# A two-layer graph kernel: layer 1's self connection four pairs later, and eight groups' bases that stay in SBUF

## What is computed

```python
x = layernorm(x + L0_gnn(x, a, src, dst, edge_attr_4, edge_attr_64, ...))
x = layernorm(x + L1_gnn(x, a, edge_attr_16, edge_attr_4, src, dst, ...))

# inside L1_gnn
sc = concat([x0 @ Wsc0 * a * inv8, einsum(x1, Wsc1) * a * inv32])  # self connection, every node
e0, e1 = f0[edge_src], f1[edge_src]                                # gather per edge
...                                                                # messages from edge weights
n = segment_sum(message, edge_dst) / cnt                           # scatter to nodes
return sc + alpha * conv                                           # conv, alpha from n
```

## Time and profile before

| | us |
|---|---|
| median of 3 runs | 2022.29 |
| the runs | 2023.46, 2022.29, 2012.63 |
| profiled execution, its time | 2024.94 |
| profiled execution, its span | 2023.2 |
| stage 1, about | 0 to 722 |
| stage 2, about | 722 to 1048 |
| stage 3, about | 1048 to 1760 |
| stage 4, about | 1760 to 2023 |

### The profile page before, as it was taken

How to read it: one execution, slowest core, us unless ns; L and a number is a source line. 1 busy time by engine, 2 the same in 40 slices (tenths; PEclk the granted TensorE clock), 3 DMA queues, 4 the chain that set the end, 5 groups by cost and what they waited for, 6 DMA issues and landing times.

```text
span 2023.2 us, 47391 instructions
## 1 busy us (share of the span) xinstructions
PE 1423.3 (70%) x10327; PEld 1269.9 (63%) x10327; DVE 1445.6 (71%) x5762; ACT 1059.0 (52%) x3502; POOL 1473.4 (73%) x1925
## 2 busy tenths in 40 slices
PE   5888778887878668888868998898988888100000
PEld 4777677776767557667637888888888888100000
DVE  6767667776766459999955666666666666099998
ACT  3434434444433239999954554554454544056666
POOL 3777777777777548888864677777777777478886
PEclk9989988899988889999978999999999999555555
DMA  9877787777774379999944777777777776499997
GB/s 354 233 190 194 189 192 178 184 177 187 176 177 86 38 233 344 337 339 338 340 154 126 174 172 162 173 163 166 169 167 168 168 167 144 92 362 401 403 395 290
DMA packets 257604, 440.09 MB, mean 218 GB/s; under 512 B 33838, under 2 KB 131792, under 8 KB 257360
## 3 DMA queue, kind: packets, MB, share of 16 engines
q1 hardware_dynamic: 143920, 303.31, 44.1%
q0 software_dynamic: 75264, 67.79, 24.4%
q10 hardware_dynamic: 38304, 67.91, 9.1%
HBM read 235.60 MB, written 203.27 MB: 217 GB/s over the span
## 4 chain that ended last, share of the span: by engine, by line
POOL 28%; issue 20%; DVE 12%; PE 10%; DMA 7%; ACT 6%; ACTq 1%; DVEq 1%; another core or an unknown queue 1%; POOLq 0%; SPq 0%
POOL table L563 14%; POOL xg L538 8%; DVE stats L1186 4%; DVE res L1147 3%; DMA table<-sums,row_all 3%; ACT y L938 3%; POOL half_rstd L602 3%; DMA xg<-x_rows,src_all 2%; DVE res L1136 1%; DMA xg<-in_x_rows,src_all 1%; PE ps L711 1%; PE ps L731 1%; PE ps L697 1%; PE ps L713 1%
## 5 line engine op out<-in xcount | busy, mean ns | idle before, releaser
L563 POOL DMA_INDIRECT table<-sums,row_all x392 | 631.8, 1612 | 254.7 <-issue 143.2
L938 ACT ACTIVATE y<-res,norm 128x160 f32<-128x160 f32 x756 | 330.3, 507 | 129.6 <-POOL norm L604 72.8
L873 ACT COPY msg<-ps 128x192 f32<-128x192 f32 (+1 forms) x196 | 57.6, 294 | 576.4 <-PE ps L731 348.5
L538 POOL DMA_INDIRECT xg<-in_x_rows,src_all x196 | 200.2, 1022 | 86.3 <-issue 55.4
L1096 DVE SCALAR_TENSOR_TENSOR x1g<-ps,a_all,x1g 128x160 f32<-128x160 f32 x392 | 132.4, 379 | 163.0 <-PE ps L752 133.2
L538 POOL DMA_INDIRECT xg<-x_rows,src_all x196 | 195.3, 996 | 64.2 <-issue 59.4
L1186 DVE BATCH_NORM_STATS2 stats<-res 128x6 f32<-128x160 f32 x784 | 196.0, 312 | 3.8 <-issue 0.3
L1052 DVE TENSOR_TENSOR pe<-ps,ea_all 128x192 f32<-128x192 f32 x196 | 70.1, 357 | 173.2 <-ACT msg L873 98.4
L661 PE MATMUL ps<-ident,xg 128*128 128x128 f32 x392 | 87.3, 306 | 147.2 <-ACT xz L860 108.8
L711 PE MATMUL ps<-weights,midT 128*128 128x128 f32 (+1 forms) x784 | 164.3, 293 | 35.0 <-DVE msg L1057 23.3
L602 POOL TENSOR_TENSOR half_rstd<-var,minus_half 128x8 f32<-128x8 f32 x98 | 164.7, 1680 | 14.2
(11 more groups left out here) (127 smaller groups left out, 4462.6 us busy)
## 6 DMA issues: line engine op xcount, KB each, us to landing
table<-zeros SPq DMA_DIRECT2D x98, 384.0 KB
tab<-table SPq DMA_DIRECT2D x98, 384.0 KB, 5.2
table<-zeros SPq DMA_DIRECT2D x49, 648.0 KB
tab<-table SPq DMA_DIRECT2D x98, 324.0 KB, 5.4
xzT<-in_xzT SPq DMA_DIRECT2D x98, 320.0 KB, 5.0
x1g<-x_rows SPq DMA_DIRECT2D x98, 320.0 KB
base_rows<-x1g SPq DMA_DIRECT2D x98, 320.0 KB
x1g<-base_rows SPq DMA_DIRECT2D x98, 320.0 KB, 5.0
```

What stands on the lines that cost most here:

```text
L538: pool.indirect_dma_start(out=xg[j % RING][:, t, 0:width], out_offset=None, in_=rows, in_offset=bass.IndirectOffsetOnAxis(ap=src_all[:, at ...
L563: pool.indirect_dma_start(out=table[l], out_offset=bass.IndirectOffsetOnAxis(ap=row_all[:, at:at + 1], axis=0), in_=sums[j % 4][:, t, 0:W] ...
L938: last = nc.scalar.activation(y[u][:, t, :], res[u][:, t, :], ACT.Identity, scale=rstd[u][:, t:t + 1], bias=shift[u][:, t:t + 1])
```

## The change

In stage 3 the self connection's parts get a lag four steps greater on every engine: on PE `nodes1a` and `nodes1b` 6 for 2 and `turn1a` and `turn1b` 5 for 1, on ACT `copy_z1` 4 for 0 and `copy_nTa`, `copy_nTb` 5 for 1, on DVE `add_self_a`, `add_self_b` 6 for 2, on SP `load_x1` 4 for 0 and `store_base` 8 for 4. `store_base` leaves out groups 90 to 97: their bases are left in the eight `x1g` buffers. The last stage takes the groups in the order 96, 97, 90 to 95, then 0 to 89 (`at_last`), so that item m uses the buffer its group already lies in; `load_base` leaves out the first eight items, and `table_row1` waits for these on the self connection's last count in place of a load. ACT's list of the last stage is written out for 18 steps at each end, for 10 before.

```diff
+def at_last(m):
+    if isinstance(m, int) and m < RING:
+        return NG - 2 + m if m < 2 else NG - RING + m - 2
+    return m - RING
...
                 def store_base(g, m, u):
+                    if isinstance(m, int) and m >= NG - RING:
+                        return
...
-                    run_stages(sp, base, NP, 10, [(10, pair_landed), (4, store_base), (0, load_x1),
+                    run_stages(sp, base, NP, 10, [(10, pair_landed), (8, store_base), (4, load_x1),
                                                   (0, load_attr), (0, load_dst_row)], RING)
...
                 def load_base(g, m, u):
+                    if isinstance(m, int) and m < RING:
+                        return
...
-                                 base_rows[bass.ds(m * GROUP, GROUP), :]...
+                                 base_rows[bass.ds(at_last(m) * GROUP, GROUP), :]...
...
                     for u in range(RING):
-                        sp.wait_ge(s_bstore[u], landed(2 * NG - RING + (u - 2 * NG) % RING, first_of(u, RING), RING))
+                        sp.wait_ge(s_bstore[u], 16 * len(range(first_of(u, RING), 2 * NG - RING, RING)))
                     run_stages(sp, NG, NG, 10, [(0, load_base), (2, load_table)], RING)
...
-                    run_stages(pe, NP, NP, 10, [(1, first_map), (0, hidden), (1, edge_weights), (2, nodes1a), (0, turn_x),
-                                                (1, turn1a), (3, second_map), (2, turn_mid), (1, turn1b),
-                                                (2, nodes1b), (5, sum_pair)], RING)
+                    run_stages(pe, NP, NP, 10, [(1, first_map), (0, hidden), (1, edge_weights), (6, nodes1a), (0, turn_x),
+                                                (5, turn1a), (3, second_map), (2, turn_mid), (5, turn1b),
+                                                (6, nodes1b), (5, sum_pair)], RING)
...
                     run_stages(act, NP, NP, 10, [(0, copy_z), (1, copy_h), (0, hidden_act), (0, copy_xT),
-                                                 (1, copy_nTa), (3, copy_message), (2, copy_midT), (0, copy_z1),
-                                                 (1, copy_nTb), (5, copy_sums)], RING)
+                                                 (5, copy_nTa), (3, copy_message), (2, copy_midT), (4, copy_z1),
+                                                 (5, copy_nTb), (5, copy_sums)], RING)
...
-                run_stages(act, l * NG, NG, 10 if l else 18, ([(8, normalise), (9, store), (0, gates)] if l == 0 else [(9, store), (8, normalise)]), RING)
+                run_stages(act, l * NG, NG, 18, ([(8, normalise), (9, store), (0, gates)] if l == 0 else [(9, store), (8, normalise)]), RING)
...
-                        (4, message_vectors), (2, compare), (4, message_sum), (2, add_self_a), (1, products), (2, add_self_b)], RING)
+                        (4, message_vectors), (2, compare), (4, message_sum), (6, add_self_a), (1, products), (6, add_self_b)], RING)
...
                 def table_row1(g, m, u):
-                    dve.wait_ge(s_base[u], landed(g, first_of(u, RING), RING))
+                    if isinstance(m, int) and m < RING:
+                        dve.wait_ge(s_z1, 2 * NG)
+                    else:
+                        dve.wait_ge(s_base[u], landed(g - RING, first_of(u, RING), RING))
```

More of the change, by code:

```diff
@@ L472, in load_base @@
                     sp.dma_start(x1g[u][:, :, :].rearrange("p t c -> p (t c)"),
-                                 base_rows[bass.ds(m * GROUP, GROUP), :].rearrange("(p t) c -> p (t c)", t=T)).then_inc(s_base[u], 16)
+                                 base_rows[bass.ds(at_last(m) * GROUP, GROUP), :].rearrange("(p t) c -> p (t c)", t=T)).then_inc(s_base[u], 16)
                 def load_table(g, m, u):
@@ L486, in load_table @@
                     sp.dma_start(tab2[u // 2][:, u % 2, 0:T * W],
-                                 table[l][bass.ds(m * GROUP, GROUP), :].rearrange("(p t) c -> p (t c)", t=T)).then_inc(s_nx[u], 16)
+                                 table[l][bass.ds((at_last(m) if l else m) * GROUP, GROUP), :].rearrange("(p t) c -> p (t c)", t=T)).then_inc(s_nx[u], 16)
                 def store_last():
@@ L494, in store_last @@
                         sp.wait_ge(s_yrest, SHARED * l + m - (NG - SHARED) + 1)
-                        sp.dma_start(to[m * GROUP:(m + 1) * GROUP, :].rearrange("(p t) c -> p (t c)", t=T),
+                        n = at_last(m) if l else m
+                        sp.dma_start(to[n * GROUP:(n + 1) * GROUP, :].rearrange("(p t) c -> p (t c)", t=T),
                                      y[u][:, :, :].rearrange("p t c -> p (t c)")).then_inc(s_store[u], 16)
@@ L613, in factor @@
                     pool.wait_ge(s_q2, g + 1 - NG)
-                    tt(q[:, 1, :, :], a_all[:, bass.ds(m - 1, 2), :], q[:, 1, :, :], ALU.mult).then_inc(s_q3, 2)
+                    tt(q[:, 1, :, :], a_all[:, bass.ds(at_last(m) - 1, 2), :], q[:, 1, :, :], ALU.mult).then_inc(s_q3, 2)
                     pool.wait_ge(s_q3, g + 1 - NG)
@@ L949, in store @@
                     to = x1_rows if l == 0 else out
-                    act.dma_start(to[bass.ds(m * GROUP, GROUP), :].rearrange("(p t) c -> p (t c)", t=T),
+                    act.dma_start(to[bass.ds((at_last(m) if l else m) * GROUP, GROUP), :].rearrange("(p t) c -> p (t c)", t=T),
                                   y[u][:, :, :].rearrange("p t c -> p (t c)")).then_inc(s_store[u], 16)
-                run_stages(act, l * NG, NG, 10 if l else 18, ([(8, normalise), (9, store), (0, gates)] if l == 0 else [(9, store), (8, normalise)]), RING)
+                run_stages(act, l * NG, NG, 18, ([(8, normalise), (9, store), (0, gates)] if l == 0 else [(9, store), (8, normalise)]), RING)
         @block.vector
```

## The result

| | before | after |
|---|---|---|
| median, us (12 runs each) | 2016.86 | 2006.06 |
| runs, us | 2006.83 to 2028.18 | 1996.94 to 2011.11 |
| profiled execution, its time | 2024.94 | 2009.39 |
| its span | 2023.2 | 2007.6 |

A forecast was written before the change was run, and what follows sets the result against it. It took POOL's scatters to pace stage 3 and ACT the last stage; 7.5 + 3.8 + 0.2 = 11.5 us off 2024.94 gave 2013.4, less 2.65 for the runs' median 2010.8, said as 2011, range 2000 to 2021.

The forecast's parts named there:

- Start of the last stage: Border of stages 3 and 4: two tables load first instead of after four bases, DVE starts 3.8 us earlier.
- Start of stage 3: Ahead of POOL's first scatter: less self connection work lets it start 7.5 us earlier, bounds 2.7 to 19.3.
- the 6.5 us: PE's self connection work taken out of the steps of pairs 2 to 5 ahead of the first sum, counted in full.
- unnamed waits: ACT's waits at stage 3's start with no cause in the profile, 10.8 us in sum; expected to stay, over by 1074.
- the unknown part: Stage 3's start, ahead of PE's steps: x1 loads moved behind and ACT's waits; 0 to 12.8 us, taken as 1.0.
- First to last scatter: Stage 3 from POOL's first scatter to its last: 660.7 us should stand, within 5.
- Last stage: ACT bounds it at 2.53 us a group; eight base loads fewer give nothing, more written-out groups 0.2 us.
- The unnamed waits going with the copies: Rival, stage 3's start: ACT's waits vanish with the moved copies, 17 to 19 us there, 2000 us in all; chance 0.12.
- The DMA engines as the bound: Rival, last stage: DMA engines set the pace, so fewer base loads give 6.5 us more, 2004.5; chance 0.06.
- More collisions: Rival, stage 3: among the first ten pairs five more scatters wait 1.7 us, 8.5 us back, 2019; chance 0.08.
- a slow jump of ACT's loop: Rival, last stage: ACT's loop waits at its jump back in each of ten rounds, 34 us, 2045; chance 0.06.
- The small gain at stage 3's start: Rival: PE's half clock and the gather burst eat all but 0 to 3 us there, 2017 in all; chance 0.18.

The follow-up runs named there:

- bases_only: Changed kernel with the self connection's lags set back, the last stage still taking eight groups' bases from SBUF; ratio to the kernel before 0.999.
- before_again: Kernel before plus one line: POOL waits for ACT's copy of pair j-2 at gathers 3 to 7 of stage 3; ratio to the kernel before 0.995.
- short_burst: Changed kernel with POOL waiting for PE at five pairs' gathers of stage 3, so 8 instead of 18 leave together; ratio to the kernel before 0.9886.
- the repeat: Changed kernel run once more as it is; ratio to the kernel before 0.9947, first to last scatter 639.3 us.
- no_base_loads: Changed kernel without any load of a base in the last stage; ratio to the kernel before 0.9929, last stage 240.2 us.
- late_store: Changed kernel with ACT issuing each store of the last stage one group later; ratio to the kernel before 0.9918.

## Why the prediction was right, and where it was off

**The size.** 11.5 us foreseen, 11.5 measured by the ratio (7.7 to 15.3). That is 0.57%, little above the 0.5% that was to count as faster, and the interval (0.38 to 0.76%) holds that limit. But the terms that the experiments bear out come to 4.5 + 4.3 = 8.8 us: the agreement to a tenth is luck, that it lies in the interval is not. The time itself, 2006.06, lies 5 us under the 2011 foreseen and just inside the forecast's own range, since the kernel before has 2016.86 as its median over 12 runs where the prediction started from 2022.29 over 3.

**Start of the last stage**, 3.8 us with bounds 3.4 to 4.6: 3.95 in the two profiles, 4.3 between the kernel before and bases_only. The working holds: two tables in front instead of four bases, DVE 4.75 us after the landing (4.9 foreseen). The prediction weighed a fixed 2.0 us plus the bytes at 436 GB/s (the Trainium skill, DMA: Bandwidth & Descriptors, Anatomy of one DMA; the section gives this fit for transfers that GpSimd issues, and these are SyncE's), an estimate of 3.5 us for two tables. By the same fit one table, 0.33 MB, is an estimate of 2.8 us, and the first landed 2.73 us after its issue (1748.38 to 1751.11). The second table landed 4.1 us after the first was issued (1748.38 to 1752.48), but with six table loads issued in 2.70 us, not two, so it does not separate the two estimates.

**Start of stage 3**, 7.5 us with bounds 2.7 to 19.3: 4.3. This is the term that was mis-sized. The step that failed is "PE runs without a gap through nearly all of these steps, so I count them in full", together with PE's lower clock, which the prediction named as a cost of up to 3.8 us and put at nothing in the sum. Two parts of the 6.5 us did not come.

The first is the self connection of the first group. It lay inside ACT's unnamed waits: in the earlier trace rows two of them stand ahead of just those copies, and the waits' end, 25 us after the first gather, did not move. Work taken out ahead of that moment only makes the waits longer (14.5 for 11.9 us).

The second is the first step behind the waits. Steps of PE can be counted from `first_map` of one pair to that of the next. `first_map` of pair 2 starts 28.07 us after the first gather before, 27.01 now. The three steps from there to pair 5 took 5.01, 5.00 and 6.48 us before and take 5.52, 3.17 and 4.55 now, so they give -0.5, +1.8 and +1.9 us. With the 1.1 ahead of them that is the 4.3 measured. The step that gave nothing ran for the most part at PE's lower clock. Windows of it before and now, then of the next step now:

```profile
1077.14:1082.15 5.01, 5.01 (x45) 4.75 (x44) 3.60 (x15) 2.74 (x11) 0.00 (x0) 1.00 0.54 159
```

```profile
1072.60:1078.12 5.52, 5.52 (x26) 4.77 (x26) 3.73 (x19) 2.11 (x8) 0.00 (x0) 0.58 0.00 1
1078.12:1081.29 3.17, 3.17 (x27) 2.85 (x26) 2.45 (x11) 2.30 (x9) 0.00 (x0) 1.00 0.00 0
```

The same list of instructions took 5.52 us at a mean clock of 0.58 and 3.17 at 1.00, so the clock cost about 2.35 us. In the kernel before, PE's clock rose for good 25.1 us after the first gather, with bases_only 24.4. In the seven profiles with the lags and the burst of 18 it rose 30.6 to 32.5 us after it, and this step took 5.25 to 6.10 us. PE had been idle for 4.89 us just ahead of the step, where before it had worked since 1069.47, 5.1 us ahead of the waits' end. That the later rise goes with the lags is shown by bases_only; that the idle time is its reason is argued only.

A small part came unforeseen. The third step of before holds the 0.37 us wait for edge attributes shown above. It made that step some 0.6 us longer. The prediction had read the 5.59 us as PE's work alone and put SP's earlier loads at nothing; now the wait is gone.

With the burst shortened the lags are worth 4.9 to 7.0 us, and in before_again and short_burst PE's clock is 1.00 from 12 us after the first gather on. The 6.5 of PE's rows was a fair price for the work, in the wrong place. That the waits would swallow an earlier start was said, and used to cut the unknown part to 1.0; it should have been applied to the known part too.

**Unnamed waits**: foreseen to stay and be over by 1074; they ended at 1071.4 and grew. Shown is that their length goes with the number of gathers issued without a pause, under either order of the self connection, and that the x1 loads are not their cause. Not shown is the path by which POOL's gathers hold ACT back; the records place the delay mostly between PE's recorded end and the semaphore's update.

**First to last scatter**: foreseen to stand within 5; the profile said -4.3, and the repeat showed the spread of this stretch to be some 20 us. No part of it can be given to the change.

**Last stage**: even waits of 0.77 us and a DMA share of 1.03, as foreseen. no_base_loads shows that the DMA engines do not bound it, late_store that ACT does; but ACT's lead over DVE is 2.6 us in 241. The eight more written-out groups gave nothing, as POOL fed the first ones no faster (waits of 1.00 to 1.56 us on `norm`).

**The rivals.** The unnamed waits going with the copies: no, they grew. The DMA engines as the bound: refuted by no_base_loads. More collisions: no sign, nor a slow jump of ACT's loop, whose 77 waits are none above 0.8 us; a rule of the Trainium skill (Runtime: NRT & Kernel Launch, Instruction fetch mechanics) that a far jump forces a fetch did not show in the time here. The small gain at stage 3's start came half true: its two reasons, the lower clock and the burst, are what held the gain to 4.3 us, against its 0 to 3.

## What to carry to other kernels

Before counting removed work as time won, find the moment at which the next wait ends for a reason of its own; only what lies behind that moment counts. Then ask at which clock PE will run what is left: less work ahead of a stretch can leave it slower there. A busy share near 1 of an engine or of the queues doesn't make it the bound: look for who waits for whom, and ask how far behind the next engine is before pricing a cure for the first. And compare the stages, not the spans: two executions of one kernel differed here by more than the whole change brought.

## What the runs showed of the hardware

A burst of indirect gathers on POOL held up ACT, whose operands were ready by PE's recorded ends. With 18 in a row (1.25 us each, 22.4 us) ACT lost 12 to 16 us and was free 2.2 to 3.4 us after the burst. Spreading them out was worth 9 to 11.5 us at the head of the stage, as much as the 8.8 us of the change's own terms or more.

PE's granted clock is at the lower of its two levels, 1.2 and 2.4 GHz, for much of the stretch in which ACT's waits leave PE idle, and at the higher one in the same stretch with the short burst. Windows of the changed kernel, then of short_burst:

```profile
1060.00:1070.00 10.00, 4.32 (x17) 3.34 (x17) 0.00 (x0) 0.67 (x3) 6.16 (x7) 0.66 0.26 63
```

```profile
1060.00:1070.00 10.00, 9.77 (x70) 8.18 (x71) 7.64 (x37) 5.95 (x23) 6.19 (x7) 1.00 0.23 57
```

PE is busy 4.3 of 10 us at a mean clock of 0.66, and 9.8 of 10 at 1.00. Four weight products took 1.22 us at 1063.39 and 0.61 at 1081.29, so part of what the short burst gives comes through the clock: an estimate from the step above is 2.4 us of the 11.5. The two were not separated by a run.
